# Three of sixteen heads turned by TensorE instead of the DMA, in a local attention kernel

## The reference

```python
x = x + 0.5 * ffn(layernorm(x), w_up, w_down)      # ternary weights, RMS norms, exact gelu
x = x + attention(layernorm(x), Wq, Wk, Wv, Wo)    # 16 heads of 64
x = x + 0.5 * ffn(layernorm(x), w_up, w_down)

# attention, per block of 128 queries and per head:
k_cat = [k of the block before, own, after, and of 128 sums of 16 tokens each (side)]
v_cat = the same of v
logits = q @ k_cat.T + (0 where |key - query| <= 127 or side, else -1e9)
m = max(max(logits), 0)
probs = exp(logits - m) / (sum(exp(logits - m)) + exp(-m))
y = probs @ v_cat ; out = y @ Wo
```

## Time and profile before

| what | value |
|---|---|
| median of 3 runs | 2499.99 us (2496.33 to 2504.56) |
| profiled execution, its own time | 2508.59 us |
| its span, first to last instruction | 2506.5 us |
| instructions | 98603 |
| busy over the span: TensorE, ScalarE, VectorE, GpSimd | 88%, 85%, 76%, 65% |
| mean granted TensorE clock | 0.978 of 2.4 GHz |
| DMA queue that carries the transposes | 294.00 MB, 77.9% of 16 engines' span |

### The profile page before, as it was taken

The page is one execution under the profiler, slowest core; times in us unless marked ns, Lnnn a source line. Parts: engine busy times, 40 slices in busy tenths (PEclk is TensorE's granted clock), DMA queues, the critical chain, the costliest instruction groups (busy, mean ns, idle before and its releaser), DMA issues. The chain is left out here.

```text
span 2506.5 us, 98603 instructions
## 1 busy us (share of the span) xinstructions
PE 2198.1 (88%) x34394; PEld 1693.7 (68%) x34394; DVE 1893.7 (76%) x4448; ACT 2140.6 (85%) x4422; POOL 1638.5 (65%) x1453
## 2 busy tenths in 40 slices
PE   1888885899899889999988998998899999979998
PEld 0555553677777767777776777777677777746666
DVE  6789986687687767777776876877677777758876
ACT  2988882899899879989987998998799899869998
POOL 1677775577677657767765776776576677647765
PEclk9999996999999999999999999999999999989999
DMA  5100000999999999999999999999999999911001
GB/s 186 49 0 0 0 1 18 144 160 159 146 162 162 160 141 160 160 148 163 163 159 140 161 162 149 162 158 156 144 162 156 158 158 160 157 32 34 33 25 42
DMA packets 1111389, 300.24 MB, mean 120 GB/s; under 512 B 1091440, under 2 KB 1109872, under 8 KB 1110896
## 3 DMA queue, kind: packets, MB, share of 16 engines
q1 hardware_dynamic: 1110896, 294.00, 77.9%
HBM read 14.68 MB, written 8.39 MB: 9 GB/s over the span
## 5 line engine op out<-in xcount | busy, mean ns | idle before, releaser
L987 POOL TENSOR_TENSOR probs_split<-probs,probs_split 128x512 f16<-128x512 f32 (+1 forms) x1026 | 1156.6, 1127 | 578.8 <-ACT probs_split L1267 577.2
L1313 DVE CUSTOM_DVE_ANT_0 score_ps<-score_ps,mask,neg_qk_scale 128x512 f32<-128x512 f32 (+1 forms) x1028 | 750.0, 730 | 337.1 <-PE score_ps L1091 319.8
L1267 ACT ACTIVATE probs_split<-probs 128x512 f16<-128x512 f32 (+1 forms) x1026 | 632.3, 616 | 133.9 <-ACT probs L1252 93.8
L1252 ACT ACTIVATE probs<-score_ps,minus_max 128x512 f32<-128x512 f32 (+1 forms) x1027 | 683.4, 665 | 54.9 <-DVE minus_max L1313 49.4
L1109 PE MATMUL y_ps<-v_parts,probsT 128*128 128x64 f16 x11922 | 520.1, 194 | 96.7 <-DMA probsT<-probs_split 93.3
L1109 PEld LDWEIGHTS y_ps<-v_parts,probsT 128*128 128x128 f16 x11922 | 455.8, 98 | 215.1 <-DMA probsT<-probs_split 157.2
L1088 PE MATMUL score_ps<-k_parts,q_parts 64*128 64x128 f16 (+1 forms) x4524 | 420.7, 235 | 30.7 <-issue 25.1
L1091 PE MATMUL score_ps<-k_parts,q_parts 64*128 64x128 f16 (+1 forms) x4524 | 420.7, 235 | 0.0
L1088 PEld LDWEIGHTS score_ps<-k_parts,q_parts 64*128 64x128 f16 x4524 | 279.2, 94 | 73.9 <-issue 35.8
L1091 PEld LDWEIGHTS score_ps<-k_parts,q_parts 64*128 64x128 f16 x4524 | 279.2, 94 | 0.0
L1020 PE MATMUL item_ps<-b_xT,wk_split 128*128 128x128 f16 x3168 | 223.0, 221 | 13.3 <-DVE b_xT L1305 6.5
(11 more groups left out here) (173 smaller groups left out, 3969.2 us busy)
## 6 DMA issues: line engine op xcount, KB each, us to landing
probsT<-probs_split SPq DMA_TRANSPOSE x1033, 4.1
out_x<-x_resident SPq DMA_DIRECT2D x16, 512.0 KB, 2.9
x_resident<-in_L_attn_x SPq DMA_DIRECT2D x14, 512.0 KB, 4.3
raw_up<-in_L_ffn_w_up SPq DMA_DIRECT2D x1, 1024.0 KB, 5.7
raw_down<-in_L_ffn_w_down SPq DMA_DIRECT2D x1, 1024.0 KB, 7.6
raw_q<-in_L_attn_Wq SPq DMA_DIRECT2D x1, 1024.0 KB, 9.5
raw_k<-in_L_attn_Wk SPq DMA_DIRECT2D x1, 1024.0 KB, 11.5
raw_v<-in_L_attn_Wv SPq DMA_DIRECT2D x1, 1024.0 KB, 13.2
```

The costliest lines, as they stand in the source:

```text
L987: nc.gpsimd.tensor_tensor(parts_of[v % NPARTS][:, LO, cols], probs[v % NBUF][:, cols], parts_of[v % NPARTS][:, HI, cols], ALU.subtract).th ...
L1252: nc.scalar.activation(probs[v % NBUF][:, cols], score_ps[v % NBUF][:, cols], ACT.Exp, bias=bias[:, j % 2, h:h + 1], scale=-1.0, accum_out ...
L1267: nc.scalar.activation(parts_of[v % NPARTS][:, HI, cols], probs[v % NBUF][:, cols], ACT.Copy).then_inc(phi_done.sem, 1)
L1313: nc.vector.tensor_tensor_reduce(out=score_ps[v % NBUF][:, cols], in0=score_ps[v % NBUF][:, cols], in1=w.mask[:, cols], scale=w.neg_qk_sca ...
```

## The change

The probabilities of heads 1, 12 and 13 of every block no longer go through the split, GpSimd and the DMA. TensorE transposes their four f32 tiles into a PSUM bank that holds nothing at the time (`PT1` and `PT13`: the first `y_ps` bank; `PT12`: the `item_ps` bank that `V0` takes next), behind the values of steps 0, 11 and 12. ScalarE's `high` and VectorE's `low` then read the bank and write the two parts straight into `pt`, as they do for other items. So SP, GpSimd and `split_high` pass over these heads; their counts go by the 13 others. Exponentials four heads later wait for the turn's `item_done` in place of GpSimd's low part. New waits on TensorE: each turn waits for its bank, the values of head 0 and of the three heads for the low parts, `YT0` for that of `PT13`, `V0` for that of `PT12`. `SK1` now stands ahead of `PT1` in the finished list of step 0.

```diff
--- before.py
+++ after.py
@@ -714,21 +714,25 @@
 
 
 
-    V1, Q0, XTR, Q1, K0, YT1, K1, OUTP, YT0, V0 = PLAIN = range(10)
-    SK0, SK1, SV0, SV1 = range(10, 14)
-    FIRST_ORDER = [SK1, V1, Q0, XTR, Q1, SV1, K0, YT1, K1, OUTP, YT0, V0]
-    LAST_ORDER = [V1, Q0, XTR, Q1, K0, YT1, K1, SK0, OUTP, YT0, V0, SV0]
-
-    PIECES = [[(V1, 0)], [(V1, 1)], [(Q0, 0)], [(Q0, 1)], [(XTR, 0), (Q1, 0)], [(Q1, 1)], [(K0, 0)], [(K0, 1), (YT1, 0)],
-              [(K1, 0)], [(K1, 1)], [(OUTP, 0)], [(OUTP, 1)], [(OUTP, 2)], [(OUTP, 3)],
+    PT1, V1, Q0, XTR, Q1, K0, YT1, K1, PT12, PT13, OUTP, YT0, V0 = PLAIN = range(13)
+    SK0, SK1, SV0, SV1 = range(13, 17)
+    FIRST_ORDER = [SK1, PT1, V1, Q0, XTR, Q1, SV1, K0, YT1, K1, PT12, PT13, OUTP, YT0, V0]
+    LAST_ORDER = [PT1, V1, Q0, XTR, Q1, K0, YT1, K1, SK0, PT12, PT13, OUTP, YT0, V0, SV0]
+
+    PIECES = [[(V1, 0), (PT1, 0)], [(V1, 1)], [(Q0, 0)], [(Q0, 1)], [(XTR, 0), (Q1, 0)], [(Q1, 1)], [(K0, 0)], [(K0, 1), (YT1, 0)],
+              [(K1, 0)], [(K1, 1)], [(OUTP, 0)], [(OUTP, 1), (PT12, 0)],
+              [(OUTP, 2), (PT13, 0)], [(OUTP, 3)],
               [(YT0, 0), (V0, 0)], [(V0, 1)]]
     XTR_SLOT = 4
     FIRST_SIDE = {0: SK1, 5: SV1}
     LAST_SIDE = {9: SK0, 15: SV0}
-    TURNS = (XTR, YT1, YT0)
+    BY_PE = {1: PT1, 12: PT12, 13: PT13}
+    TURNS = (XTR, YT1, YT0, PT1, PT12, PT13)
     KEYS, QUERIES, VALUES = (K0, K1, SK0, SK1), (Q0, Q1), (V0, V1, SV0, SV1)
     SECOND = (K1, Q1, V1, SK1, SV1, YT1)
-    N_PIECES = {k: 1 if k in TURNS else 4 if k == OUTP else 2 for k in range(14)}
+    N_PIECES = {k: 1 if k in TURNS else 4 if k == OUTP else 2 for k in range(17)}
+    TURNED_HEAD = {kind: h for h, kind in BY_PE.items()}
+    PROBS_TURNS = tuple(BY_PE.values())
     NI = len(PLAIN)
     RING = 4
     SIDE = RING
@@ -823,7 +827,7 @@
                 self.first, self.last = (isinstance(i, int) and i == 0), (isinstance(i, int) and i == ROUNDS - 1)
                 self.round = b * ROUNDS + i
                 self.heads = self.round * U
-                self.eights = self.round * (U // NPARTS)
+                self.splits = self.round * (RING * (H - len(BY_PE)))
                 self.halves = self.round * (2 * RING)
                 self.blocks = self.round * RING
                 sides = b * 4 + (0 if self.first else 2)
@@ -856,8 +860,10 @@
 
             def place(self, j, kind):
 
+                if kind == PT12:
+                    return self.place(j, V0)
                 if kind in TURNS:
-                    return y_ps[int(kind != YT0)], None
+                    return y_ps[int(kind in (XTR, YT1))], None
                 prefix = LAST_ORDER if self.first else [*PLAIN]
                 order = [*prefix, *(k for o in self.orders for k in o)]
                 at = len(prefix) + self.offset(j, kind)
@@ -871,7 +877,7 @@
             def __init__(self):
                 self.first = self.last = False
                 self.heads, self.halves, self.blocks = NBLK * H, NBLK * 2, NBLK
-                self.eights = NBLK * H // NPARTS
+                self.splits = NBLK * (H - len(BY_PE))
                 self.items = PRE_ITEMS + 4 * BATCH + NI * NBLK
                 self.his = PRE_ITEMS + 4 * BATCH + (NI - 1) * NBLK
 
@@ -894,7 +900,10 @@
         def finished(at, j, h):
 
             side = side_item(at, j, h)
-            return [(j, k) for k, piece in PIECES[h] if piece == N_PIECES[k] - 1] + ([(j, side)] if side else [])
+            pieces = [(j, k) for k, piece in PIECES[h] if piece == N_PIECES[k] - 1]
+            if side == SK1:
+                return [(j, side), *pieces]
+            return pieces + ([(j, side)] if side else [])
 
         def due(at, u):
 
@@ -940,7 +949,15 @@
 
         def turn_count(at, v):
 
-            return (at.eights + v // NPARTS + 2) * 16
+            j, h = divmod(v, H)
+            n = v % NPARTS
+            each = sum(k not in BY_PE for k in range(n, H, NPARTS))
+            return (at.blocks * each + j * each + sum(k not in BY_PE for k in range(n, h + 1, NPARTS)) + 1) * 16
+
+        def by_dma(at, v):
+
+            j, h = divmod(v, H)
+            return at.splits + j * (H - len(BY_PE)) + sum(k not in BY_PE for k in range(h))
 
         def half(v):
             return (v % H) // (H // 2)
@@ -949,7 +966,9 @@
         def _(sp):
             def turn_probs(at, v):
 
-                plo_done.wait(sp, at.heads + v)
+                if v % H in BY_PE:
+                    return
+                plo_done.wait(sp, by_dma(at, v))
                 separate(sp)
                 pv_done.wait(sp, at.heads + v - NBUF)
                 separate(sp)
@@ -982,8 +1001,10 @@
 
             def split_low(at, v):
 
+                if v % H in BY_PE:
+                    return
                 cols = columns(place_of(at, v))
-                phi_done.wait(pool, at.heads + v)
+                phi_done.wait(pool, by_dma(at, v))
                 nc.gpsimd.tensor_tensor(parts_of[v % NPARTS][:, LO, cols], probs[v % NBUF][:, cols],
                                         parts_of[v % NPARTS][:, HI, cols], ALU.subtract).then_inc(plo_done.sem, 1)
 
@@ -1044,6 +1065,14 @@
                 pe.wait_ge(xn_done, n + 1)
                 for k in range(KD):
                     last = nc.tensor.transpose(bank[:, k * P:(k + 1) * P], xn[:, k * P:(k + 1) * P], w.ident32[:])
+                last.then_inc(item_done, 1)
+
+            def turn_probs(at, v, bank):
+
+                exp_done.wait(pe, at.heads + v)
+                for t in range(4):
+                    last = nc.tensor.transpose(bank[:, t * P:(t + 1) * P], probs[v % NBUF][:, t * P:(t + 1) * P],
+                                               w.ident32[:])
                 last.then_inc(item_done, 1)
 
             def turn_y(h, e):
@@ -1099,10 +1128,13 @@
 
                 j, h = divmod(v, H)
                 if h == 0:
-                    pe.wait_ge(lo_done, at.before(j))
+                    pe.wait_ge(lo_done, at.item(j, PT1) + 1)
                 if h == H // 2:
                     pe.wait_ge(lo_done, at.item(j, YT1) + 1)
-                pe.wait_ge(turned[v % NPARTS], turn_count(at, v))
+                if h in BY_PE:
+                    pe.wait_ge(lo_done, at.item(j, BY_PE[h]) + 1)
+                else:
+                    pe.wait_ge(turned[v % NPARTS], turn_count(at, v))
                 out = y_ps[half(v)][:, (h % 8) * DH:(h % 8 + 1) * DH]
                 passes = [(t, slot, a, b) for t, slot in tiles_of(at, v) for a, b in ((HI, HI), (HI, LO), (LO, HI))]
                 for n, (t, slot, a, b) in enumerate(passes):
@@ -1121,7 +1153,20 @@
                     y_done.wait(pe, at.halves + 2 * j - 1)
                     turn_x(bank, at.blocks + j + 2)
                     return
+                if kind == PT1:
+                    pe.wait_ge(lo_done, at.item(j - 1, YT0) + 1)
+                    turn_probs(at, H * j + 1, bank)
+                    return
+                if kind == PT12:
+                    pe.wait_ge(lo_done, at.item(j, PT12))
+                    turn_probs(at, H * j + 12, bank)
+                    return
+                if kind == PT13:
+                    y_done.wait(pe, at.halves + 2 * j)
+                    turn_probs(at, H * j + 13, bank)
+                    return
                 if kind == YT0:
+                    pe.wait_ge(lo_done, at.item(j, PT13) + 1)
                     turn_y(0, at.halves + 2 * j)
                     return
                 if kind == YT1:
@@ -1129,7 +1174,10 @@
                     turn_y(1, at.halves + 2 * j - 1)
                     return
                 if 0 in pieces:
-                    bank_free(index, gap)
+                    if kind == V0:
+                        pe.wait_ge(lo_done, at.item(j, PT12) + 1)
+                    else:
+                        bank_free(index, gap)
                 if kind == OUTP:
                     project_out(bank, at.item(j, YT1), pieces)
                 elif kind in (SK0, SV0):
@@ -1168,7 +1216,7 @@
                         block_item(at, b, j, side, (0, 1))
                     values(at, u - PV_LAG)
                     for kind, piece in PIECES[h]:
-                        if kind in (YT0, YT1):
+                        if kind in (YT0, YT1, *PROBS_TURNS):
                             block_item(at, b, j, kind, (piece,))
 
             pe.wait_ge(cleared, CLEARED)
@@ -1191,6 +1239,8 @@
             c = int(kind in SECOND)
             if kind == XTR:
                 return xt[xt_parity][:, :, part, :]
+            if kind in PROBS_TURNS:
+                return pt[TURNED_HEAD[kind] % NBUF][:, 4 * part:4 * part + 4, :]
             if kind in KEYS:
                 return kr[:, slot, part, 512 * c:512 * c + 512]
             if kind in QUERIES:
@@ -1202,7 +1252,7 @@
         def result(kind, bank):
             if kind == XTR:
                 return bank[:, 0:KD * P].rearrange("p (k n) -> p k n", k=KD)
```

(10 more changed lines are left out.)

## The result

The changed kernel takes 2548.68 us (median of 4 runs, 2542.04 to 2549.68) where the kernel before takes 2498.87, run beside it: ratio 1.0191, 95% interval 1.0171 to 1.0212. It is slower by 48 to 50 us; 28 us faster was forecast.

The account below looks back on a forecast made before the run. ScalarE (25.9 us) and the DMA queue (26.1) were taken to pace the 27.40 us block; afterwards TensorE: 25.9 + 0.43 + 0.28 + 0.2 + 0.2 = 27.0, 28 us less over 64 blocks, 2472 us, range 2440 to 2520.

Parts of the forecast that it names:

- TensorE has slack: In the attention phase TensorE needs 24.5 us of a 27.40 us block, 2.9 us below the pace, which show as waits.
- a pace of 1.63 us a turn: SP's DMA issues: 16 turns take 26.1 us a block; three fewer make 21.2 us, so the queue stops being a pace.
- 2.2 us a block of waiting for the DMA chain: TensorE's remaining wait in the 27.40 us block, after its 24.5 of work and 0.43 and 0.28 of other waits.
- 0.2 for the DMA: TensorE's waits for turned probabilities after the change, in us a block, with landings expected nearer 3.0 us than 4.1.
- 0.28 for the low parts of items: TensorE's waits for low parts of q, k and xT, us a block, taken to stay unchanged.
- 0.2 for new waits: All waits the turns add in TensorE's order, us a block, with 0 and 0.9 as bounds.
- the seven long waits: TensorE's waits for nothing in the profile, at seven places, 25.1 us in all, 0.43 a block, taken to stay.
- a condition: New waits are covered because TensorE's order is behind ScalarE's; without that cover they count in full.
- TensorE's own work: Three groups of four f32 transposes at 0.48 us, 1.44 us a block, bringing TensorE from 24.5 to 25.9, the new pace.
- the DMA's latency: Rival at the values' wait for the DMA: chain length counts, 13 of 16 waits stay, 33 us slower, 2533; chance 0.13.
- point of decision: The slower rival decides once TensorE's waits left and new exceed 0.8 us a block.
- The clock: Rival on TensorE: 22 transposes a block lower the granted clock, 0.3 us a block or 20 us, 2492; chance 0.05.

Follow-up runs that it names:

- e9: Kernel before plus twelve f32 transposes a block of the identity on TensorE, unread, at steps 0, 12 and 13: 2522.0 us, 1.0079.
- e4: Kernel before with the DMA transposes of heads 1, 12 and 13 left out and their values not waiting; splits and low parts stay: 2468.9 us, 0.9875.
- e8: Kernel before with heads 1, 12 and 13 neither split nor turned by any engine, their low parts left out too: 2457.0 us, 0.9821.
- e10: Changed kernel with denominators as a one-input reduction, and the two parts of the three turned heads cut to one column in 128: 2510.1 us, 1.0045.
- e5: Changed kernel with sums and extra logits in one tensor, so the denominators are a one-input reduction: 2520.8 us, 1.0076.
- e11: Changed kernel with one-input denominators and only head 13 turned by TensorE: 2532.9 us, 1.0126.
- e13: Changed kernel with one-input denominators and only head 1 turned by TensorE: 2506.6 us, 1.0012.
- e12: Changed kernel with one-input denominators and head 12's turn one step later, at step 12 beside head 13's: 2545.0 us, 1.0162.
- e7: Changed kernel with head 12 given back to split, GpSimd and DMA; heads 1 and 13 still by TensorE: 2532.9 us, 1.0136.
- e14: Changed kernel with one-input denominators and only heads 1 and 13 turned by TensorE: 2501.4 us, 0.9991.

## Why the prediction was wrong, point by point

**What bounds the kernel.** That TensorE has slack was right: e9 puts 92 us of work on it for 20. That the DMA queue is a pace of 1.63 us a turn was not: I read the pitch of a stretch that kept up with the block as the queue's capacity. In the same trace, from 1197.95 us on, 16 issues follow each other in 24.5 us, 1.53 each, so a block's 16 turns fit into 24.5 us and not only into 26.1. Leaving three turns out does help (e4, 31 us), but e4 takes away the wait of three heads for a landing as well as load on the queue, and the landings of the others take 3.9 us in the median instead of 4.1. Which of the two the 31 us are is open.

**The step that failed: that 2.2 us a block of waiting for the DMA chain could be taken away while the other waits stay.** The sum left 0.2 for the DMA, kept 0.28 for the low parts of items and had 0.2 for new waits. The first came true: 3.8 us in 1610, 0.07 a block. The other two did not: steps 3, 5 and 11 alone wait 1.48 us a block. With that the sum closes: 25.9 + 0.36 (the seven long waits, 20.6 us) + 0.07 + 0.25 (the waits for q and k) + 1.48 = 28.06 us, against 28.0 measured. The forecast made 128 us of relief (2.0 x 64); the relief measured alone is 45 us (e8). The waits for probabilities were also cover for the turn of x and for K0: with three DMA turns left out and nothing added, these two wait 1.05 us a block more (e4). I named this as a condition ("if that is gone, they count in full"), but kept 0.28 us, from rows in which they were still covered.

**TensorE's own work** was priced right, 0.48 us a turn against 0.47, 92 us. Next to the relief it lengthens the kernel by 56 us, from relief alone (0.9821) to relief and turns (1.0045, e10); these 56 hold the wait for K1 too.

**New waits, 0.2 us a block.** The turn of head 12 waited 0.56 us, inside the upper bound of 0.9 for the three together; I had seen 0.2 in one block, and the row was taken while TensorE was late. I had added VectorE's time from durations of before, so the denominators counted 0.33 us; at their new place they take 1.07. That the low part of head 1's turn moves them was missed: I cost what the change adds to VectorE, not what it pushes. It is 29 us (after against e5).

**The sum in the same terms**, in us: relief -45 (forecast -128), turns +56 (+92), reading out +8 and hold +29 (together +13). These are steps along one chain of runs (before, e8, e10, e5, after), so they add up to the measured +48 whatever their shares are; that they do proves nothing. Another order gives other shares: the turns first cost 20 us (e9), and the relief behind them (e10 against e9) is worth 9. Relief and added work use the same slack, which is why the forecast couldn't price them apart and add.

**Arithmetic.** The forecast terms make -23 us. The prediction's 26.97 us a block, and so its 28 us, do not come out of them: 25.94 + 0.43 + 0.28 + 0.2 + 0.2 is 27.05, which is 2477 us, still faster. (Eight times 2.92 is 23.4, not 23.3, and 27.4 less 25.9 is 1.5, not 1.4.)

**The rivals.** The slower side was put on the DMA's latency with 0.13. The time is near its 2533, the mechanism isn't: waits for the DMA fell to 3.8 us. Its point of decision, 0.8 us a block of waits left and new, was right: the table has 1.48. The clock did nothing.

**The signs.** Most signs of being right were there in a slower kernel: waits for turned probabilities 3.8 us (under 30 asked), ScalarE 86% (85), turns at 0.47 us (0.5), TensorE 94% (95), the DMA share down to 0.82 (0.9). The one that spoke was among those of being wrong: waits on low parts past 50 us. They are 58.0 (25.7 + 17.9 + 7.7 + 6.7), without the 8.0 for y.

**Left open.** Why head 1 is the good place is only argued: its gap in the DMA's run stands just ahead of steps 2, 4 and 6, where e11 has its waits (1.26 to 1.32 us a step in the mean against 1.02 in the median). Half of e11's waits for the DMA stand there, 35.4 of 70.8 us, and in e13, with head 1 by TensorE, 3.4 of 55.4; what the others wait for was not varied. And which loop of waits sets the 27.25 us of an undisturbed block in after isn't proved; e12 only shows that one wait in it can be taken out with no gain.

## What to carry to other kernels

A wait row names where an engine waits, not what it would gain: price a relief by leaving the work out, since the next wait in the ring may be there already and covered (e4, e8). A relief and an added cost that meet the same slack can't be priced apart (e8, e9). When an engine in a hand-written order gets one more instruction, list what comes behind it and what that will now meet on another engine; here an addition of eight columns met GpSimd's operation and cost more than half of what the loss came to. A step that got longer is not yet a wait of the instruction that is new in it: look which instruction has the idle time ahead of it (e7, e14). And in a ring of five engines waits change places: the one that e12 took out came back at other steps, and the kernel was 22 us slower.

## What of the hardware was not expected

VectorE's `tensor_tensor` and `tensor_scalar` on 128x8 f32 in SBUF take up to 1.14 and 1.15 us instead of 0.16 while GpSimd's `tensor_tensor` runs, and end 0.02 to 0.03 us after it; `tensor_reduce` on 128x16 takes 0.16 us always. f32 transposes of 128x128 follow each other on TensorE every 0.11 us, with 0.47 us for four and the change to the next matmul.
